# Attention over stored edge counts of all node pairs, in place of fetches edge by edge

## The reference, cut to what matters

```python
qk = x @ qk_w.T + qk_b
v = x @ v_w.T + v_b
scores = jnp.sum(qk[dst] * qk[src], axis=-1) / math.sqrt(v.shape[-1])
scores = jnp.clip(scores, -5.0, 5.0)
seg_max = jax.ops.segment_max(scores, dst, num_segments=n)
e = jnp.exp(scores - seg_max[dst])
seg_sum = jax.ops.segment_sum(e, dst, num_segments=n)
attn = e / seg_sum[dst]
out = jax.ops.segment_sum(attn[:, None] * v[src], dst, num_segments=n)
out = out @ o_w.T + o_b
```

## Time and profile before

| what | us |
|---|---|
| median of 3 runs (lowest, highest) | 17427.73 (17410.49, 17435.44) |
| the profiled execution | 17432.58 |
| its span, first to last instruction | 17430.9 |
| busy in the span: PE / PEld | 11606.9 / 7493.8 |
| busy: DVE / ACT / POOL | 6501.1 / 3473.3 / 6206.8 |
| mean granted TensorE clock | 0.787 |

### The profile page before, as it was taken

The page is one execution under the profiler, slowest core; times in us unless marked ns, Lnnn a source line. Parts: engine busy times, 40 slices in busy tenths (PEclk is TensorE's granted clock), DMA queues, the critical chain, the costliest instruction groups (busy, mean ns, idle before and its releaser), DMA issues.

```text
span 17430.9 us, 310182 instructions
## 1 busy us (share of the span) xinstructions
PE 11606.9 (67%) x67022; PEld 7493.8 (43%) x67023; DVE 6501.1 (37%) x30915; ACT 3473.3 (20%) x9727; POOL 6206.8 (36%) x6084
## 2 busy tenths in 40 slices
PE   2444444444545555577777666767767999999999
PEld 2222222223444444445555555555555444444443
DVE  6776767664333333333333333333333000000000
ACT  1333333331000000102222222222221000000000
POOL 2000000002544455408888888888882000000000
PEclk8666565665555555589999999999996999999999
DMA  2222222222111111153333333333334898989888
GB/s 91 88 86 87 88 88 85 87 86 67 35 35 34 34 35 35 28 222 42 42 42 41 41 41 41 42 41 42 41 42 42 333 342 332 342 332 343 331 341 308
DMA packets 1177920, 2115.02 MB, mean 121 GB/s; under 512 B 404317, under 2 KB 1020528, under 8 KB 1076672
## 3 DMA queue, kind: packets, MB, share of 16 engines
q1 hardware_dynamic: 828200, 1822.93, 29.8%
q0 software_dynamic: 348960, 284.02, 11.5%
HBM read 1647.56 MB, written 458.86 MB: 121 GB/s over the span
## 4 chain that ended last, share of the span: by engine, by line
PE 41%; issue 29%; POOL 13%; DVE 8%; another core or an unknown queue 3%; DMA 1%; DVEq 1%; ACT 1%; SPq 1%; POOLq 0%; ACTq 0%
PE ps L1371 13%; PE ps L1087 7%; POOL G L470 7%; PE ps L1376 7%; POOL reverse L786 5%; PE ps L1126 3%; PE ps L1116 2%; DVE hots L1696 2%; DVE hots L1694 1%; PE ps L1106 1%; DVE hots L1695 1%; DMA reverse<-SD,sidx 1%; PE ps L1313 1%; POOL scatter_hold L785 1%
## 5 line engine op out<-in xcount | busy, mean ns | idle before, releaser
L1087 PE MATMUL ps<-hots 128*128 128x392 f16 x4859 | 1688.3, 451 | 2009.6 <-issue 1756.3
L786 POOL DMA_INDIRECT reverse<-SD,sidx x1660 | 2647.4, 1595 | 389.4 <-issue 376.3
L1371 PE MATMUL ps<-chunk,feat 128*128 128x512 f16 (+1 forms) x10192 | 2278.9, 375 | 14.4 <-DVE feat L2011 13.5
L468 POOL TENSOR_TENSOR hold_out<-hold_in 128x1 f32<-128x1 f32 x166 | 78.3, 472 | 5334.6 <-DMA idx<-index_table 4267.7
L816 ACT ACTIVATE stagebuf<-ps 128x392 f32 x3248 | 1448.0, 504 | 2284.0 <-PE ps L1090 2229.1
L1087 PEld LDWEIGHTS ps<-hots 128*128 128x128 f16 x4859 | 638.5, 131 | 2771.1 <-issue 2694.0
L470 POOL DMA_INDIRECT G<-h_table,idx x1660 | 1654.1, 996 | 493.1 <-issue 487.8
L470 POOL DMA_INDIRECT G<-kv_table,idx x1660 | 1597.0, 962 | 517.9 <-issue 517.9
L1865 DVE TENSOR_TENSOR acc<-acc,ps 128x132 f32 x1660 | 485.4, 292 | 3144.1 <-PE ps L1237 3017.2
L1234 PE MATMUL ps<-MS,OH 128*128 128x128 f32 x3320 | 781.6, 319 | 1267.7 <-issue 865.4
L1694 DVE TENSOR_SCALAR hots<-count_lo,key_lo 128x128 f16<-128x128 f16 x4859 | 1200.9, 247 | 1122.5 <-PE ps L1090 1122.5
(11 more groups left out here) (394 smaller groups left out, 18003.0 us busy)
## 6 DMA issues: line engine op xcount, KB each, us to landing
chunk<-adj SPq DMA_DIRECT2D x720, 1792.0 KB, 9.0
adj<-stagebuf SPq DMA_DIRECT2D x406, 784.0 KB, 5.3
chunk<-adj SPq DMA_DIRECT2D x60, 1232.0 KB, 7.2
G<-in_edge SPq DMA_DIRECT2D x1660, 32.0 KB
G<-kv_table,idx POOLq DMA_INDIRECT x1660
G<-h_table,idx POOLq DMA_INDIRECT x1660
reverse<-SD,sidx POOLq DMA_INDIRECT x1660
reverse<-acc SPq DMA_DIRECT2D x4, 3225.0 KB, 20.0
```

The source lines that it names most:

```text
L786: nc.gpsimd.indirect_dma_start(reverse[j % R], bass.IndirectOffsetOnAxis(sidx[:, j:j + 1], 0), SD[:, j % R, :], None, compute_op=ALU.add). ...
L1087: nc.tensor.matmul(ps[:, bass.ds(held["to"][j % STEPW], 2 * COMBS)], hots[:, j % BRING, 0:P], hots[:, j % BRING, P:P + 2 * COMBS], start=F ...
L1371: nc.tensor.matmul(bank[k % 2][:, 0:cols], feat[0][:, hi, 0:2, :].rearrange("p a d -> p (a d)"), columns(chunk4, i % DRING, m, cols), star ...
```

## The change

The query vectors of all nodes (`qT`, 64 x 6272, and 224 overflow columns fetched by two row fetches) and the value rows with a one (`vtab`) stay on chip, in float32. For each of the 13 groups and each of the 49 source blocks (637 passes, written out without a loop; the first group has 352 columns, the others 512) TensorE takes the scores of all pairs, ScalarE the exponential, VectorE clips it to exp(-5) and exp(5) and multiplies by the stored counts, and TensorE multiplies by the values, with a second small product that counts degrees. Overflow columns are folded in at the end of a group. The 1660 row fetches from `kv_table`, 83 index fetches, the one-hots and the bfloat16 split of this stage are gone. The memsets of `S` and `MS` move behind the attention; the update stage counts on the semaphores of `node` (only names). Rings: 3 banks of scores (SB), 4 buffers after the exponential (EB), 3 weighed (WB), 3 banks of sums (AB), 2 chunks of counts (ARING).

```diff
+NI = NB * 13
+SB, EB, WB, AB, ARING = 3, 4, 3, 3, 2
+LOW, HIGH = math.exp(-5.0), math.exp(5.0)
...
@@ SyncE
-            store(kv_table, big_kv, 1, KV)
-            fetches(passes(0))
+            store(first_table, Hf, 1, D)
+            for i in range(NGRP * UCH):
+                n, c = divmod(i, UCH)
+                width = GRP if n else GCOLS // BLK
+                if i >= ARING:
+                    sp.wait_ge(att["used"], i - ARING + 1)
+                sp.dma_start(chunkA[:, i % ARING, 0:width * RUN],
...
@@ GpSimd
-            gather(pool, passes(0), 0, kv_table, KV, att["msg"], 0, per=GR)
+            pool.wait_ge(att["slots"], 3)
+            for d in range(2):
+                nc.gpsimd.indirect_dma_start(slot_rows[:, d, :], None, first_table,
+                                             bass.IndirectOffsetOnAxis(slot_of[:, d:d + 1], 0)).then_inc(tile_rows[0], 16)
...
@@ ScalarE
+            def exp(i):
+                act.wait_ge(att["score"], i + 1)
+                if i >= EB:
+                    act.wait_ge(att["weighed"], i - EB + 1)
+                cols = 512 if i >= NB else GCOLS
+                nc.scalar.activation(expo[:, i % EB, 0:cols], bank[i % SB][:, 0:cols], ACT.Exp, scale=1.0 / D ** 0.5)\
+                    .then_inc(att["exp"], 1)
...
@@ TensorE
+            def att_mul(k):
...
+                for n in range(blocks if k < NQ else 0):
+                    nc.tensor.matmul(bank[2 + k % 2][:, n * D:(n + 1) * D], turnA[:, k % 2, n * P:(n + 1) * P], qkv[:, D:2 * D],
+                                     start=True, stop=True)
+                nc.tensor.matmul(bank[4 + k % 2][0:D, 0:blocks * P], qkv[:, 0:D], turnA[:, k % 2, 0:blocks * P],
+                                 start=True, stop=True).then_inc(node["product"], 1)
...
+            def score(i):
+                n, hi = divmod(i, NB)
+                at_, cols = ORDER[n] * 512, 512 if n else GCOLS
+                if i >= SB:
+                    pe.wait_ge(att["exp"], i - SB + 1)
+                nc.tensor.matmul(bank[i % SB][:, 0:cols], qT[:, hi * P:(hi + 1) * P], qT[:, at_:at_ + cols], start=True, stop=True)\
+                    .then_inc(att["score"], 1)
+
+            def gain(i):
+                n, hi = divmod(i, NB)
+                cols, to = 512 if n else GCOLS, bank[SB + n % AB]
+                pe.wait_ge(att["weighed"], i + 1)
+                if hi == 0 and n >= AB:
+                    pe.wait_ge(att["out"], n - AB + 1)
+                nc.tensor.matmul(to[:, 0:cols], vtab[:, hi, :], weighed[:, i % WB, 0:cols], start=hi == 0, stop=False,
+                                 skip_group_check=True).then_inc(att["gained"], 1)
+                c, m = divmod(hi, CCH)
+                return nc.tensor.matmul(to[D:P, 0:cols], degw[:, :], chunkA[:, (n * UCH + c) % ARING, 0:cols * CCH]
+                                        .rearrange("p (k c e) -> p k c e", c=CCH, e=BLK)[:, :, m, :],
+                                        start=False, stop=False, skip_group_check=True)
...
+            for i in range(NI + SB - 1):
+                if i < NI:
+                    score(i)
+                if i < SB - 1:
+                    continue
+                n, hi = divmod(i - SB + 1, NB)
+                last = gain(i - SB + 1)
+                if hi % CCH == CCH - 1 or hi == NB - 1:
+                    last.then_inc(att["used"], 1)
...
+                if n >= 2 and hi == 8:
+                    att_back(0 if n == 2 else n - 1)
...
+                if hi == NB - 1 and n >= 1:
+                    att_fold(n)
...
@@ VectorE
+            def clip(i):
+                cols, e = 512 if i >= NB else GCOLS, expo[:, i % EB, :]
+                v.wait_ge(att["exp"], i + 1)
+                nc.vector.tensor_scalar(e[:, 0:cols], e[:, 0:cols], LOW, HIGH, ALU.max, ALU.min).then_inc(att["clipped"], 1)
+
+            def weigh_(i):
...
+                if m == 0:
+                    v.wait_ge(att_loaded[q % ARING], 16 * (q // ARING + 1))
+                v.wait_ge(att["clipped"], i + 1)
+                if i >= WB:
+                    v.wait_ge(att["gained"], i - WB + 1)
+                counts_ = chunkA[:, q % ARING, 0:cols * CCH].rearrange("p (k c e) -> p k c e", c=CCH, e=BLK)[:, :, m, :]
+                nc.vector.tensor_tensor(weighed[:, i % WB, 0:cols].rearrange("p (k e) -> p k e", e=BLK),
+                                        expo[:, i % EB, 0:cols].rearrange("p (k e) -> p k e", e=BLK), counts_, ALU.mult)\
+                    .then_inc(att["weighed"], 1)
...
+            for i in range(NI + 1):
+                if i < NI:
+                    clip(i)
+                if i == 0:
+                    continue
+                weigh_(i - 1)
+                n, hi = divmod(i - 1, NB)
+                if n >= 1 and hi == 14:
+                    if n == 1:
+                        att_hot(0)
+                    att_hot(n)
...
+                if n >= 2 and hi == 12:
+                    att_sum(0 if n == 2 else n - 1)
...
+            nc.vector.memset(MS[:, :, :], 1.0)
+            link(nc.vector.memset(S[:, :, :], 1.0))
```

## The result

The changed kernel takes **15953.06 us** (median of 4 runs, 15947.69 to 15954.17), the kernel before 17431.57 us beside it: ratio 0.9153, 95% interval 0.9138 to 0.9169. The forecast was 15583 us, in a range of 15430 to 16150. The range holds the time; of the gain of 1850 us that was forecast, 1478 us came and some 370 us are missing. The profiled execution took 15954.17 us, with a span of 15952.5 us.

The account below looks back on a forecast made before the run. It took GpSimd's row fetches and a round trip through the slot to bound the old edge loop. Preparing 60, loop 1374 and memsets 1.6 make 1435.6 us against 3285.3, so 17432.6 falls to 15583 us, range 15430 to 16150.

Parts of the forecast that it names:

- The sign: Whole kernel: faster by over 0.2% (35 us) with chance 0.98, slower 0.02, the same 0.00.
- Full clock from the first 10 us: New attention stage: granted clock at 1.00 from the first ten microseconds, giving 15583 us; chance 0.71.
- Rival (a): New passes: 64-row scores keep half clock throughout, 3.95 us a pass, about 16733 us; chance 0.14.
- rival (b): New passes: the clock rises and falls, half of the time each, about 16150 us; chance 0.05.
- 2.14 us a pass: TensorE in the new loop: score 0.96, gain 0.96 and degrees 0.22 us, bounds 1.94 to 2.28; 1330 us in all.
- The chain on VectorE: New passes: exponential 0.69, clip 0.42, product 0.69 and three handovers of 0.10, 2.10 us, just covered by TensorE's 2.14.
- Preparing, 60 us: Before the passes: transposes and node and query products in 12 lots of four blocks, plus smaller terms, 60 us.
- Chunks at nothing: Loads of counts in the loop: each lands in 9.0 us with 15.0 us available at the shortest, costing nothing.
- Overflow rows at nothing: Two fetches while preparing: issued at the start, needed some 50 us later, costing nothing; about 13 us if uncovered.
- Memsets, 1.6: Memsets moved behind the attention loop cost 1.6 us there; new ones of like size in front balance them, so +1.6 us.
- 13.7 us are the round trip through the slot: Old edge loop: of each 38.74 us period of 20 steps, GpSimd's fetches take 25.0 us, the slot's round trip 13.7.
- (d) no overlap: New passes: if scores did not run ahead, 6.05 us a pass at half clock, 18038 us, slower by 605; chance 0.02.

Follow-up runs that it names:

- the warm-up run: The changed kernel with 16 unused products of 128 rows by 512 float32 columns on TensorE just before the loop's first pass: 15769.28 us.
- the order two by two: The changed kernel with TensorE issuing score, score, gain, gain, degrees, degrees for two passes instead of score, gain, degrees for each: 15637.27 us.
- the last kernel: The changed kernel with 128-row scores, degrees in runs of up to 14, VectorE weighing right after each clip, scores and gains one by one: 15458.97 us, ratio 0.8872.
- the run whose clock never rose: The changed kernel with the products that fold in overflow rows cut to 1 column: 17077.0 us, one run.

## Why the prediction was right, and where it was off

The sign, the stage, and what covers what were right. It was the size of two terms that failed, in equal parts. The forecast loop was 1374 us, the measured one 1738.3: 364 us more, nearly all of what is missing.

1. **"Full clock from the first 10 us"** (the term with chance 0.71): 397 us at 0.50 instead, 182 us by the warm-up run. The prediction looked at the right rows and drew the right doubt, that a busy TensorE alone does not bring the clock. It then gave the new pass the benefit of its two full-height products in three. The runs say: one gain and one product of degrees between two 64-row scores are not enough; four products of 112 rows in a row, three of 128 and 352 columns, a warm-up, or the order two by two are; and once it is up, the same passes keep it at 1.00 for 1305 us. Rival (a) came nearest to the mechanism, for the first 397 us, but height is not all of it: the clock rose with 64-row scores taken two by two, and stayed at 0.50 in the kernel without fetches, where all products have 128 rows. Of rival (b) the stage has the two levels; it rose once and did not swing.
2. **"2.14 us a pass"**, bounds 1.94 to 2.28: 2.445, above the upper bound. (2.445 - 2.14) x 621.7 = 190 us, where the warm-up run leaves 1556.3 - 1374 = 182. I had priced each float32 switch at 0.10 from the earlier trace rows, "nothing" at the low end, and the switch to and from the degrees at 0. By difference between runs: the change between 64 and 128 rows costs 0.195 a pass (2.445 to 2.25), the two switches of the degrees' 64 float16 columns 2.25 - 1.955 = 0.295, and score to gain at equal height 0.00. The 1.06 of the earlier trace rows was the right time for each of the two float32 products (1.06 and 1.05), where the upper bound had 1.06 and 1.00, and the bound left out the third switch (0.33 instead of 0.22). The Trainium skill ("TensorE: Matmul & The Clock Gate", Part 2, "Step-by-step: what each phase is for") says that a load is pulled ahead of products in flight if its row groups do not conflict with theirs or it goes to the background buffer. The traces show it where neighbours are alike (the last kernel's load for the gain at 5001.60 is at 5001.18) and not in the changed kernel (load and product both at 4999.92); by the rule alone either could have gone ahead.
3. **The chain on VectorE**, "2.10 us, just covered": right. Exponential 0.60, clip 0.43 and product 0.69 us; leaving out the clip gave nothing. Its weak place was real, and it cost 99 / 621.7 = 0.16 us a pass as soon as scores and gains took 0.86 us each.
4. **Preparing, 60 us**: 58. **Chunks at nothing**: 6.7 us to land, no wait. **Overflow rows at nothing**: fetched at 4082 to 4084, needed at 4125.6. **Memsets, 1.6**: the stretch from the sums to the convolution grew from 108.5 to 110.6 us. The later stages' other 8 us are not the change's: its second trace has 15931.4 - 5860.1 = 10071.3 us there, the kernel before 10072.1.
5. **What bounded the kernel before.** "13.7 us are the round trip through the slot" was a wrong reading of a right row. GpSimd's wait for VectorE came behind the stall, in which TensorE and VectorE stood idle at "issue" while GpSimd went on; without the stall it passes the same barrier with no wait. The sum did not suffer, since it took the stage's measured 3285.3 us off whole, and the stall goes with the fetches. But it doesn't always occur: the same change is worth 1478 us with it and 457 us without. The forecast says nothing of that. On executions of the second kind its range would still have held the time, but its gain of 1850 us would have been four times too large: that the comparison fell on the kind of the first trace was luck.
6. **(d) no overlap**: at half clock the pass is 4.57 us, below the 5.12 us from which the change loses against the kernel with the stall. Against the other one (stage from 4068.7 to 6320.9, 58 us of it preparing) the break-even is (2252.2 - 58) / 621.7 = 3.5 us a pass, and the run whose clock never rose (17077 us) is slower than that kernel (16412.63 us). The mishap that I gave 0.02 stood closer than it looked.

Open: what the engines lack in the stall, and why it comes with the fetches in some sets of runs and not in others. No experiment here brought it about. The two kinds never mix within a set, and the three sets of experiments ran on three different chips (kernel before: 16412.63, 16391.96 and 17424.77 us), so whether the chip or the time decides is not known. Open too is what lifts the clock: the runs give four cases that do and two that don't, and neither height nor busy time alone separates them.

## What to carry to other kernels

Look at the granted clock of a stretch beside its busy share, and at which products stand next to each other: here 16 useless products ahead of the loop were worth 182 us in it, and the order two by two brought the clock up 9 us into it. Give the stationary operands of a tight loop one height and type where zero rows are free, and run the odd ones (degrees) in batches: 0.49 us of a pass of 2.445 went that way. When the engine that binds gets faster, look again at the order on the next one; and before a wait is called a round trip, look at what the engine waited for was itself doing.

## What the runs showed of the hardware that I had not expected

- TensorE 2858.31 of 2858.50 us busy at a granted clock of 0.50, with 128-row products for more than half of it; and 1552.60 of 1577.00 us at 0.50 with 128-row products alone (the kernel before without its fetches).
- Rows filled with zeros cost TensorE nothing here: a float32 product of 512 columns takes 0.86 us at 128 rows behind its like, and 1.06 us with 64 rows between products of 128.
- The kernel before can differ by 6% from set to set (17424.77 and 16391.96 us), with the same code and the same granted clock in the edge loop, while it agrees within 0.3% inside each set. The changed kernel differs by 0.1% between its two sets (15953.06 and 15934.56 us).
- The degrees' product of 512 float16 columns: 0.22 us in a run of 14 (3.14 / 14), 0.34 alone, and it makes the float32 products on both sides of it longer (0.95 and 0.96 in place of 0.86, in the kernel with 128-row scores).
